# Gated cross-attention block: attention loop written out, opening reordered with idle buffers for batch 1

## The reference, cut to what matters

```
q = rope(layernorm(x) @ Wq);  k = rope(ctx @ Wk);  v = ctx @ Wv
w = softmax(q k^T / 4)                      # per batch and head, 256 x 256
x = x + tanh(g_xattn) * ((w v) @ Wout + bout)
h = layernorm(x)
y = relu(h @ up)^2 @ down + (h @ expert_weight) * (sum of the two largest of h @ gate)
x = x + tanh(g_ffn) * (layernorm(y) * gamma + beta)
```

## Time and profile before

| | |
|---|---|
| median of 3 runs | 1626.7 us (1625.29 to 1629.2) |
| profiled execution, its own time | 1633.85 us |
| its span, first to last instruction | 1632.0 us |
| mean granted TensorE clock | 0.986 |
| busy: TensorE, VectorE, ScalarE, GpSimd | 1551.6, 973.9, 639.2, 295.3 us |

### The profile page before, as it was taken

How to read it: one execution, slowest core, us unless ns; L and a number is a source line. 1 busy time by engine, 2 the same in 40 slices (tenths; PEclk the granted TensorE clock), 3 DMA queues, 4 the chain that set the end, 5 groups by cost and what they waited for, 6 DMA issues and landing times.

```text
span 1632.0 us, 27835 instructions
## 1 busy us (share of the span) xinstructions
PE 1551.6 (95%) x9760; PEld 1154.9 (71%) x9760; DVE 973.9 (60%) x1448; ACT 639.2 (39%) x962; POOL 295.3 (18%) x370
## 2 busy tenths in 40 slices
PE   6499999999999999988999999999999999999997
PEld 4356666656666666655788787887878878788786
DVE  6578877877777787865663644535435354353524
ACT  3155555555555555556552222222222222222221
POOL 5222222221222222211000201102001021010202
PEclk9699999999999999999999999999999999999999
DMA  4724444444443444443440110101101011010101
GB/s 143 160 50 109 122 109 118 124 112 118 102 106 97 106 109 124 104 105 100 123 135 21 45 33 20 39 20 46 33 14 45 20 46 33 1 53 26 47 6 39
DMA packets 67156, 120.82 MB, mean 74 GB/s; under 512 B 12280, under 2 KB 25720, under 8 KB 67064
## 3 DMA queue, kind: packets, MB, share of 16 engines
q1 hardware_dynamic: 67064, 119.50, 27.7%
HBM read 51.17 MB, written 16.78 MB: 42 GB/s over the span
## 4 chain that ended last, share of the span: by engine, by line
PE 82%; DVE 10%; issue 4%; ACT 1%; SPq 1%; DMA 1%; POOL 1%; DVEq 0%; POOLq 0%; ACTq 0%
PE pP L962 16%; PE pA L1150 11%; PE pO L962 11%; PE pB L1150 11%; PE pT L962 10%; PE pA L1047 5%; PE pO L1075 5%; PE pM L962 4%; DVE mneg L1369 3%; PE pB L1063 2%; PE pT L969 2%; PE pP L969 2%; PE pM L969 2%; SPq L499 1%; PE pM L1117 1%
## 5 line engine op out<-in xcount | busy, mean ns | idle before, releaser
L1369 DVE TENSOR_REDUCE mneg<-pA 128x4 f32<-128x1024 f32 x250 | 305.6, 1222 | 149.3 <-PE pA L1047 147.8
L864 ACT ACTIVATE probs<-pB 128x1024 f32<-128x1024 f32 x249 | 255.3, 1025 | 264.9 <-PE pB L1063 259.7
L1472 DVE TENSOR_TENSOR relu<-relu 128x512 f32<-128x512 f32 x128 | 88.3, 690 | 256.0 <-ACT hid L915 256.0
L685 POOL TENSOR_SCALAR var_eps<-meanvar 128x1 f32<-128x1 f32 x96 | 34.7, 361 | 1064.0 <-DVE meanvar L1254 1064.0
L1150 PE MATMUL pA<-dn,hid 128*128 128x512 f32 x768 | 198.7, 394 | 0.9
L1150 PE MATMUL pB<-dn,hid 128*128 128x512 f32 x768 | 196.0, 391 | 0.0
L962 PE MATMUL pP<-fT,up 128*128 128x512 f32 x768 | 190.3, 396 | 0.0
L962 PE MATMUL pO<-fT,up 128*128 128x512 f32 x768 | 187.4, 393 | 0.0
L1150 PEld LDWEIGHTS pA<-dn,hid 128*128 128x128 f32 x768 | 143.1, 188 | 36.1 <-DVE hid L1474 4.8
L962 PEld LDWEIGHTS pO<-fT,up 128*128 128x128 f32 x768 | 144.4, 188 | 32.1 <-issue 0.2
L1150 PEld LDWEIGHTS pB<-dn,hid 128*128 128x128 f32 x768 | 144.2, 188 | 31.0
(11 more groups left out here) (188 smaller groups left out, 1963.3 us busy)
## 6 DMA issues: line engine op xcount, KB each, us to landing
stk<-kT SPq DMA_DIRECT2D x192, 128.0 KB, 2.9
stq<-qT SPq DMA_DIRECT2D x192, 128.0 KB, 3.0
fres<-x_scratch SPq DMA_DIRECT2D x34, 256.0 KB, 2.8
xin<-x SPq DMA_DIRECT2D x32, 256.0 KB, 2.8
xres<-x SPq DMA_DIRECT2D x32, 256.0 KB, 3.0
x_scratch<-xres SPq DMA_DIRECT2D x32, 256.0 KB, 2.0
out<-y_s SPq DMA_DIRECT2D x32, 256.0 KB, 2.0
fx<-x_scratch SPq DMA_DIRECT2D x29, 256.0 KB, 2.7
```

What stands on the lines that cost most here:

```text
L685: nc.gpsimd.tensor_scalar_add(var_eps[:], meanvar[:, 1:2], EPS).then_inc(ve_made, 1)
L864: nc.scalar.activation(probs[:, s % 4, :, :, :].rearrange("p a b s -> p a (b s)"), psum[:, :, :], ACT.Exp).then_inc(exp_done, 1)
L1369: nc.vector.tensor_reduce(mneg[par][:, :, 2 * u:2 * u + 2].rearrange("p t q -> p q t"), psum[:, :, :].rearrange("p q (t k) -> p q t k", t= ...
L1472: nc.vector.tensor_tensor(r[:], r[:], r[:], ALU.mult).then_inc(sq_made, 1)
```

## The change

- The attention loop is written out: every engine's program has iterations 2 to 13 (2 to 11) one after the other, without a jump and with constants in the waits.
- Batch 1's turned tiles of the opening are written to other buffers: keys into `probs` 1 and 2, queries into `av_s`. So they don't wait for batch 0's stack transfers. ScalarE waits ahead of its first exponential until batch 1's stacks are in, since it overwrites these buffers.
- The stacks of batch 0 are issued half 0 of keys and queries first, then half 1. For batch 1 the maxima rows of batch 0 are issued between the halves.
- In `OPENING`, kT1 and qT1 of batch 0 come ahead of K0 of batch 1.
- V1 and V0 of batch 0 move from steps 0 and 2 of iteration -1 to steps 5 and 7, among the maxima.
- There are two buffers `rot2`, used in turn.
- ScalarE rounds the four wq chunks ahead of the tables; GpSimd splits its two of them ahead of the second deviation.
- TensorE gets extra transposes of the identity whose result nobody reads: 22, 28 and 8 ahead of X0, K0 and Q0 of batch 0, and 5 in each step with maxima of iteration -1.

```diff
 OPENING = (
     ("X0", 0), ("K0", 0), ("Q0", 0), ("X1", 0), ("kT0", 0), ("K1", 0), ("Q1", 0),
-    ("X0", 1), ("qT0", 0), ("K0", 1), ("kT1", 0), ("qT1", 0), ("Q0", 1),
+    ("X0", 1), ("qT0", 0), ("kT1", 0), ("qT1", 0), ("K0", 1), ("Q0", 1),
...
-FIRST = {0: ("V1",), 2: ("V0",), 11: ("m0",)}
+AWAKE = {("X0", 0): 22, ("K0", 0): 28, ("Q0", 0): 8}
+FIRST = {5: ("V1",), 7: ("V0",), 11: ("m0",)}
+AWAKE_FIRST = 5
...
+        k1T = [probs[:, 1 + k, :, :, :].rearrange("p q t s -> p (q t) s").bitcast(F32R) for k in range(2)]
+        q1T = [av_s[:, KC * k:KC * (k + 1), :].bitcast(F32R) for k in range(2)]
+
+        def turned_tiles(x, b):
+
+            if opened(x + "T1", b) and b == 1:
+                return q1T if x == "q" else k1T
+            return [a[:] for a in (qT if x == "q" else kT)]
...
+        def stack_in(x, half, b):
+
+            if opened(x + "T1", b) and b == 1:
+                return second_in[x][half], STACK_DMAS * INC
+            return st_in[x][half], STACK_DMAS * INC * (1 if isinstance(b, int) and b == 0 else b)
...
-            with eng.Fori(0, (B - 4) // 2 - ahead) as trip:
-                iteration(2 * trip + 2, 0)
-                iteration(2 * trip + 3, 1)
+            for i in range(2, B - 2 - 2 * ahead):
+                iteration(i, i % 2)
...
-            for x in "kq":
-                for half in range(2):
+            for half in range(2):
+                for x in "kq":
                     load_stack(0, 0, half, x)
             load_x(2, 0)
             load_x(2, 1)
             load_ctx(2)
             for x in "kq":
-                for half in range(2):
-                    load_stack(1, 1, half, x)
+                load_stack(1, 1, 0, x)
             load_max(0, 0, 0)
+            for x in "kq":
+                load_stack(1, 1, 1, x)
...
             inv_std(1)
             split_ctx(0, 0)
+            split_weights(CC + 2, EARLY)
             inv_std(2)
-            split_weights(CC + 2, EARLY)
...
-                    if some(b) and t == 0:
+                    if some(b) and t == 0 and not opened(name, b):
                         for half in range(2):
-                            act.wait_ge(st_in[name[0]][half], STACK_DMAS * INC * b)
+                            act.wait_ge(*stack_in(name[0], half, b - 1))
...
                         if isinstance(i, int) and i == 0 and s == 0:
                             act.wait_ge(w_lo, W1 - CC - 2)
+                            for x in "kq":
+                                for half in range(2):
+                                    act.wait_ge(*stack_in(x, half, 1))
...
                 if n == 0:
-                    round_weights(CC, CC + 2)
+                    round_weights(CC, EARLY)
...
-                    round_weights(CC + 2, EARLY)
...
+            def keep_awake(count, dst=opening_banks[-1]):
+
+                for _ in range(count):
+                    nc.tensor.transpose(dst[:, 0:P], ident[:], ident[:])
...
                 for n, (name, b) in enumerate(OPENING):
+                    keep_awake(AWAKE.get((name, b), 0))
...
+                    if isinstance(i, int) and i == -1 and s >= DELAY:
+                        keep_awake(AWAKE_FIRST, pT)
...
-                    if some(len(ROPES) * b + r):
-                        dve.wait_ge(roped, len(ROPES) * b + r)
-                    nc.vector.tensor_tensor(view(rot2[:]), xv[:, :, ::-1, :], table(sin_t),
+                    if some(len(ROPES) * b + r - 1):
+                        dve.wait_ge(roped, len(ROPES) * b + r - 1)
+                    nc.vector.tensor_tensor(view(rot2[r % 2][:]), xv[:, :, ::-1, :], table(sin_t),
                                             ALU.mult).then_inc(freed, 1)
```

More of the change, by code:

```diff
@@ L234, in flamingo_gated @@
         rot_k = sb1("rot_k", [P, D])
-        rot2 = sb1("rot2", [P, D])
+        rot2 = [sb1("rot20", [P, D])]
         mT = [sb1(f"mT{i}", [NH // 2, S], F32R) for i in range(2)]
@@ L253, in flamingo_gated @@
         sin_t = sb1("sin_t", [P, NT, 2, ANG, PAIR])
+        rot2.append(sb1("rot21", [P, D]))
         rot = {"Q0": rot_q0, "Q1": rot_q1, "K0": rot_k, "K1": rot_k}
@@ L339, in flamingo_gated @@
         st_in = {x: [sem(f"st_in_{x}{h}") for h in range(2)] for x in "qk"}
+        second_in = {x: [sem(f"second_in_{x}{h}") for h in range(2)] for x in "qk"}
         a_done = sem("a_done")
@@ L492, in load_stack @@
                 slots = slice(8 * half, 8 * half + 8)
-                dst, src, parts = (st_q[par], qT, Q_PARTS) if x == "q" else (st_k[par], kT, K_PARTS)
+                dst, parts, src = ((st_q[par], Q_PARTS) if x == "q" else (st_k[par], K_PARTS)) + (turned_tiles(x, b),)
                 sp.wait_ge(*taken_of(x + "T1", b))
@@ L500, in load_stack @@
                                      src[part][low:low + PAIR * HD, :, :].rearrange("p c s -> p (c s)").bitcast(F32)
-                                     ).then_inc(st_in[x][half], INC)
+                                     ).then_inc(stack_in(x, half, b)[0], INC)
             def load_max(b, par, half):
@@ L572, in first_loads @@
                     for half in range(2):
-                        sp.wait_ge(st_in[x][half], STACK_DMAS * INC * B)
+                        sp.wait_ge(*stack_in(x, half, B - 1))
                 sp.wait_ge(taken[BANK["V0"]], number("V0", B - 1))
@@ L691, in rope_sum @@
                 t1 = rot_of(name, b)
-                nc.gpsimd.tensor_tensor(t1, t1, rot2[:], ALU.add).then_inc(roped, 1)
+                nc.gpsimd.tensor_tensor(t1, t1, rot2[ROPES.index(name) % 2][:], ALU.add).then_inc(roped, 1)
             def split_ctx(b, par):
@@ L823, in evacuate @@
                 else:
-                    if some(b) and t == 0:
+                    if some(b) and t == 0 and not opened(name, b):
                         for half in range(2):
-                            act.wait_ge(st_in[name[0]][half], STACK_DMAS * INC * b)
+                            act.wait_ge(*stack_in(name[0], half, b - 1))
                             alone(act)
+                    hi = turned_tiles(name[0], b)[0]
                     if name[0] == "q":
-                        nc.scalar.mul(qT[0][:, :, cut], turned_psum, SCALE).then_inc(made, 1)
+                        nc.scalar.mul(hi[:, :, cut], turned_psum, SCALE).then_inc(made, 1)
                     else:
-                        nc.scalar.copy(kT[0][:, :, cut], turned_psum).then_inc(made, 1)
+                        nc.scalar.copy(hi[:, :, cut], turned_psum).then_inc(made, 1)
             def take_av(b, g):
@@ L1037, in logits_a @@
                     for x in "kq":
-                        pe.wait_ge(st_in[x][s // 8], INC * STACK_DMAS * (b + 1))
+                        pe.wait_ge(*stack_in(x, s // 8, b))
                         alone(pe)
@@ L1279, in evacuate @@
                 elif name[0] in "qk":
-                    src, scale = (qT, SCALE) if name[0] == "q" else (kT, 1.0)
-                    nc.vector.scalar_tensor_tensor(src[1][:, :, cut], turned_psum, scale,
-                                                   src[0][:, :, cut].bitcast(F32),
+                    hi, lo = turned_tiles(name[0], b)
+                    nc.vector.scalar_tensor_tensor(lo[:, :, cut], turned_psum, SCALE if name[0] == "q" else 1.0,
+                                                   hi[:, :, cut].bitcast(F32),
                                                    ALU.mult, ALU.subtract).then_inc(freed, 1)
```

## The result

The changed kernel takes 1621.74 us (median of 8 executions, 1620.63 to 1622.78) against 1626.21 for the kernel before beside it. The ratio is 0.9962, 95% interval [0.9949, 0.9975]: faster by 4.5 us in the medians and 6.2 by the ratio. The forecast was 1607.0 with a range of 1601 to 1617. The direction was right; the saving was forecast at 19.7, which is three to four and a half times what came. Four single executions further down (2171 to 8394 us: one of e2, one of e6 and two of kernels before) are slow ones and stay out of the ratios and ranges.

A forecast was written before the change was run, and what follows sets the result against it. TensorE, busy 1551.6 of 1632.0 us, was taken as the bound, leaving its stalls and low-clock stretches to gain. Loop 8.2 plus opening 11.5 gave 19.7 off the median 1626.7: 1607.0, range 1601 to 1617.

The forecast's parts named there:

- Loop, 8.2 forecast: Attention loop: writing it out removes two long TensorE jumps of 4.1 us each, with in-line code costing nothing; 8.2 us saved.
- rival 2: Attention loop: the jumps' cost belongs mostly to the profiled execution or returns as a fetch stall; 11.5 alone, 1615; 9%.
- rival 4: Written-out attention loop: in-line code is fetched too late, stalling TensorE once per iteration; slower, 1644 us; 3%.
- Opening, 11.5 forecast: Start of the kernel: iteration 0 of attention begins at 69.4 instead of 80.87, saving 11.5 us.
- First stack transfer: Opening, SyncE's queue: first issue at about 28.3 instead of 35.45, from four pieces of 3.8, 1.4, 0.8 and 1.2.
- Dummies of the opening: Opening, TensorE: dummy transposes raise the clock before Q0 of batch 0, saving 1.4 us; 28 of them take 3.5.
- Maxima from 42.2: Opening, VectorE: maxima start at 42.2 rather than 62.97, once batch 0's first stack halves have landed at about 41.
- V1 and V0 "some 0.4 each": Maxima steps: V1 and V0 lie in TensorE's slack and cost VectorE some 0.4 us each at 2.4 GHz.
- That margin of 0.7 is thin: SyncE's queue: turned maxima (m0) ready at 54.7, SyncE reaching their row transfers at about 55.4.
- the new wait: ScalarE's first exponential waits until all batch 1 stacks have landed; SyncE's queue sets it, at 69.4.
- rival 1: Opening: dummies don't hold the clock up, maxima (m0) late, 1614 to 1618; mild form a late m0 alone; 15%.
- The rule on transposes: TensorE's clock gate: the skill says transposes don't count as busy; the prediction held that a trace row shows them raising it.

The follow-up runs named there:

- e2: The changed kernel with the attention loop back instead of written out; 1628.12 us, ratio 0.9977 to the kernel before.
- e6: The changed kernel with the attention loop back, run once more on another chip; 1627.60 us, ratio 0.9986 to the kernel before.
- e9: The kernel before, unchanged, run again for a second profile; 1627.05 us, ratio 0.9990.
- e12: The changed kernel with rounding and splitting of the last two wq chunks back behind tables and second deviation; 1625.37 us, ratio 0.9982 to the kernel before.
- e7: The changed kernel with no dummy transposes at all; 1619.47 us, ratio 0.9943 to the kernel before.
- e4: The changed kernel without the five dummy transposes in each maxima step, the opening's kept; 1618.43 us, ratio 0.9911 to the kernel before.
- e3: The changed kernel with batch 0's maxima rows issued behind both halves of batch 1's stacks; 1615.55 us, ratio 0.9892 to the kernel before.
- e5: The changed kernel, unchanged, run again on another chip; 1621.75 us, ratio 0.9957 to the kernel before.

## Why the prediction was wrong

**Loop, 8.2 forecast.** The term was read correctly from one execution and then taken off the median of others unchanged. The prediction said that the profiled execution was 7.15 above the median and even named the long jumps as a possible cause (rival 2, 9%). It should have followed from its own numbers: two stalls of 4.1 and an excess of 7.15 are nearly the same size, so the median execution could hardly have both stalls. e9 shows an execution without them, and from its first exponential on it is only 0.3 us longer than the changed kernel. **This is the first step that failed.** What writing out gave is 3.7 us by medians on the kernel before, and 5.9 in the changed one, where it was the stalls at the feed-forward jumps that it spared. The rule of the forecast that in-line code costs nothing held: 44.95 an iteration, so rival 4 is refuted.

**Opening, 11.5 forecast.** In the profiles 75.69 stands against 80.87, 81.50 and 82.12 for the old opening: 5.2 to 6.4. Step by step:

- *First stack transfer* forecast 28.3, measured 29.67: 5.8 of the 7.2 came. GpSimd's splits ended at 14.16, as forecast (14.2). But VectorE and GpSimd now split their wq chunks at the same time. GpSimd's two took 2.98 (2.67 in the earlier trace rows) and VectorE's two 2.90 from 11.81 on, where they take 1.28 in e12, with GpSimd's splits later. So Q0 waited for VectorE's, until 14.77: 3.3 instead of 3.8. "As late as now" for the second deviation was 1.5 too early (GpSimd's `rstd` at 16.20, in the kernel before at 14.72), and X1, which needs it, left TensorE idle for 0.8 behind Q0; it did not stay hidden.
- *Dummies of the opening*: right that they bring the clock up. The 28 at the high level took 3.22 (forecast 3.5), K0 ran in 1.68. Q0 took 3.01 instead of 4.32, but that was not theirs: without them Q0 runs in 3.00 too (e7).
- *Maxima from 42.2*: 45.13. 1.4 of this are the late start. I carried the rest of the opening on at 2.4 GHz, and K0 and Q0 of batch 1 ran partly at 1.2 GHz. Where K0 ran at the high level, with the same opening, the maxima began at 44.07 (e4) to 44.45 (e3). What decides the level there is not known.
- *V1 and V0 "some 0.4 each"*, "in TensorE's slack": 3.19 and 1.33. **This is the second step that failed**, together with the late start. V1 was priced at the high level, and the clock was low: 2.93 instead of some 1.65. V0 did run at the high level. It cost 1.33 because the five dummies had used up the slack: logits and dummies together take 1.13 a step (logits at 55.20, 56.32 and 57.45), and even the forecast's own 0.4 + 0.6 out of 1.15 left 0.15. Without the dummies V0 costs nothing and V1 1.98 (e4). The late start (2.9) and these steps (4.7) put the maxima rows at 62.3 instead of 54.7. It is the late m0 of rival 1, from another cause: the clock was low for the first maxima and V1, while behind them the dummies did hold it.
- *"That margin of 0.7 is thin"*: the queue was at the rows at 55.8 (forecast 55.4), stood 6.6 us, and what stood behind it took 13.35 to the first exponential (forecast 14.0), with 3.25 from the last transfer's issue to its landing (forecast 3.87). The mechanism of the new wait was right; the term that was mis-sized is the time of the maxima rows, and e3 gives nearly all of it back (6.2 us).

Rival 1 with its mild form ("a late m0 alone", 15% for the whole rival) is what happened in the opening, and rival 2 (9%) what happened to the loop. Each was priced with the other part intact, so neither gave 1621.7. Taken together they do: 1626.7 less some 5 to 6.

**The rule on transposes.** 22 dummies ran in 4.96, 0.23 each, and 28 behind them in 3.22, 0.115 each: the clock rose with nothing but transposes on TensorE. That contradicts, for this chip and this kernel, what the Trainium skill says (TensorE: Matmul & The Clock Gate, "Part 4: PE-mode transpose"), as the row in the prediction did. The times show it, not the granted clock: the record reads 1.00 over all of the first 14 us, also in the kernel before over a K0 that took 2.93. But the prediction took it further than the row went: between 44.8 and 47.5, with transposes and logits of 48 rows in turn and no pause, the clock stayed at 0.50. Behind V0, up to 68.5, the same work in turn had 1.00. Why the clock was down for it ahead of V1 and up behind V0 is open.

## What to carry to other kernels

A queue with several customers is only as early as its latest item: before an item is put between others, ask when its data are ready at the worst clock, and who waits for what stands behind it. A buffer taken as idle needs a wait when it is used again; put that wait at the instruction that really overwrites it, one for each part. And a saving read from a profile that lies above the median has to be checked against that excess before it is taken off the median.

## What the runs showed that I had not expected

- The kernel before has a spread of some 12 us (1623.66 to 1635.77 beside e9 to e12) that the changed one lacks (1620.55 to 1624.47 in e5), and two long jumps can be there in one execution and absent in another. With its loop back the changed kernel does not have the wide spread either (5.4 us in e2, 4.0 in e6), so the loop alone does not make it.
- In the changed kernel the form of the attention loop decides what the jumps of the feed-forward loop cost: 1.6 to 2.5 us of "issue" each in e2 and e6, none in e5.
- Dummy transposes cost real time where the engine they warm is itself in the chain: 3.3 us here, while the logits that ran faster for them (0.50 instead of 0.80) were waited for by nobody.
